# The eigen-solver beside an LSTM: rank-two vector formed in PSUM, shorter roots, counting by one instruction, selection by one-hot products

## The reference

```python
h = relu(layernorm(x)); x = x + L0(h, adj)   # A_hat h, W1, batch norm, relu, W2, batch norm
h = relu(layernorm(x)); x = x + L1(h, adj)   # two graph convolutions, then LSTMs over windows of 1 to 4 nodes
h = relu(layernorm(x)); x = x + L2(h, adj)   # U (relu((U^T h) W1 + b1) W2 + b2)
h = relu(layernorm(x)); x = x + L3(h, adj)   # three convolutions with adj * adj

# the part of L2 that the change is about
deg = sum(A, 0) + sum(A, 1) - diag(A)
d = where(deg > 0, rsqrt(deg), 0)
_, U = eigh(d[:, None] * (diag(deg) - A) * d[None, :])      # all eigenvectors of a 64x64 symmetric matrix
```

## Time and profile before

| | us |
|---|---|
| median of 3 runs | 989.73 (988.24 to 990.09) |
| the profiled execution | 988.91 |
| its span, first to last instruction | 987.1 |
| busy in the span: PE, DVE, ACT, POOL | 856.1, 571.1, 518.7, 348.2 |
| mean granted clock of TensorE | 0.962 of full |

### The profile page before, as it was taken

The page is one execution under the profiler, slowest core; times in us unless marked ns, Lnnn a source line. Parts: engine busy times, 40 slices in busy tenths (PEclk is TensorE's granted clock), DMA queues, the critical chain, the costliest instruction groups (busy, mean ns, idle before and its releaser), DMA issues.

```text
span 987.1 us, 12434 instructions
## 1 busy us (share of the span) xinstructions
PE 856.1 (87%) x3721; PEld 565.4 (57%) x3721; DVE 571.1 (58%) x3070; ACT 518.7 (53%) x958; POOL 348.2 (35%) x412
## 2 busy tenths in 40 slices
PE   2687768599899989998698879778999999999998
PEld 1344433364568536774367534566758848848846
DVE  5899867779778986779887987105104204304101
ACT  0466456466666736665466545474564454544531
POOL 1233210246555644565556556562202202202000
PEclk9999979799999999999899989898999999999999
DMA  8000000000000000000000000000000100100101
GB/s 336 0 1 1 1 0 1 1 1 1 0 1 1 1 1 1 2 0 1 0 1 1 1 1 0 1 1 1 1 0 2 43 0 1 43 0 1 43 1 43
DMA packets 2963, 13.27 MB, mean 13 GB/s; under 512 B 464, under 2 KB 464, under 8 KB 2640
## 3 DMA queue, kind: packets, MB, share of 16 engines
q1 hardware_dynamic: 2896, 12.48, 3.1%
HBM read 8.28 MB, written 4.19 MB: 13 GB/s over the span
## 4 chain that ended last, share of the span: by engine, by line
PE 61%; DVE 29%; ACT 4%; POOL 3%; issue 2%; DMA 0%; SPq 0%; DVEq 0%; ACTq 0%; POOLq 0%
PE PS L450 60%; POOL BIG L979 2%; DVE ST L1657 2%; DVE stats L1629 2%; DVE X L1833 2%; DVE Fq L1439 1%; DVE seg L1440 1%; ACT T L798 1%; DVE mv L1636 1%; DVE stats L1608 1%; ACT T L854 1%; POOL sc L948 1%; DVE sc L1173 1%; DVE vcol L1170 1%; DVE S L1190 1%
## 5 line engine op out<-in xcount | busy, mean ns | idle before, releaser
L450 PE MATMUL PS<-BIG,wts 128*128 128x512 f32 (+2 forms) x952 | 344.8, 498 | 14.2 <-POOL BIG L979 10.8
L979 POOL TENSOR_TENSOR BIG<-BIG 128x256 f32<-128x256 f32 (+2 forms) x252 | 239.2, 956 | 171.8 <-ACT BIG L888 88.0
L450 PEld LDWEIGHTS PS<-BIG,wts 128*128 128x128 f32 x952 | 179.0, 193 | 138.2 <-issue 96.8
L888 ACT ACTIVATE BIG<-PS,lbias 128x256 f32<-128x256 f32 (+2 forms) x312 | 165.5, 559 | 115.8 <-PE PS L450 113.5
L450 PE MATMUL PS<-H,wts 128*128 128x256 f32 (+2 forms) x312 | 123.0, 498 | 10.8 <-POOL H L979 7.0
L1833 DVE TENSOR_TENSOR X<-X,PS 128x512 f32<-128x512 f32 x64 | 43.3, 680 | 138.2 <-PE PS L450 87.1
L790 ACT ACTIVATE BIG<-PS 128x1024 f32<-128x1024 f32 x64 | 65.6, 1024 | 88.4 <-PE PS L450 88.4
L450 PE MATMUL PS<-T,wts 128*128 128x512 f32 x192 | 103.1, 659 | 2.2 <-ACT T L790 1.8
L790 ACT ACTIVATE T<-PS 128x512 f32<-128x512 f32 x96 | 55.8, 594 | 92.0 <-PE PS L450 91.7
L798 ACT ACTIVATE T<-X,shift,rstd 128x128 f32<-128x128 f32 x192 | 78.4, 482 | 34.6 <-DVE shift L1645 34.6
L1852 DVE TENSOR_TENSOR T<-PS,wts 128x512 f32<-128x512 f32 x16 | 11.1, 692 | 142.8 <-PE PS L450 142.8
(11 more groups left out here) (313 smaller groups left out, 1262.1 us busy)
## 6 DMA issues: line engine op xcount, KB each, us to landing
X<-x_in SPq DMA_DIRECT2D x1, 4096.0 KB, 12.7
out<-X SPq DMA_DIRECT2D x16, 256.0 KB, 2.0
wts<-w_in SPq DMA_DIRECT2D x1, 3542.0 KB, 21.4
cst<-cst_in SPq DMA_DIRECT2D x1, 419.0 KB, 3.4
AA<-adj_in SPq DMA_DIRECT2D x2, 16.0 KB, 2.0
```

The costliest lines, as they stand in the source:

```text
L450: return nc.tensor.matmul(o, l, r, start=start, stop=stop)
L888: nc.scalar.activation(LB[:, q, {"i": I_, "g": G_, "f": F_, "o": O_}[g], 0:n], PS[:, 3 * q + rank[q] % 3, 0:n], ACT.Tanh if g == "g" else ...
L979: nc.gpsimd.tensor_tensor(out, a, b, op).then_inc(pool_set[q], 1)
```

## The change

- `reflection`: before, DVE scaled the pieces of the rank-two vector into four scalars (`c2`, `vnn`, `wc`, `g0`) and used them apart. Now it adds `tn` times the row to A v in PSUM, in place (`av`), and both the next row and the update of S read that. `update` takes `pn` for `wc`.
- Inverse roots (`small_root`, and the same polynomial in `norm_roots`): the guess is one operation, followed by one Newton-like step and one step of higher order: 5 operations on single columns instead of 6 after the guess, and in the layer norm 7 instead of 9 after a guess of one instead of two.
- Grid: the tree of six additions over `Z` is one `tensor_reduce` that reads `Z` with the shift index outermost (a step of 32 elements) into `counts`. In round 0 the comparison of all counts with all lanes (2048 columns), its reduction and a copy are gone: DVE makes two 128-column tiles (`ends`, `inside`), and PE multiplies `inside` with the counts (33 columns) besides the product of before; three more single-column steps follow on DVE.
- Several operands lie in PSUM (`e_sum`, `t5`, `zb_sum`), and single-column `tensor_tensor` and `scalar_tensor_tensor` operations become `tensor_scalar` with a pointer.
- `PACE_AV` and its sisters are new, so the small products stand elsewhere between the LSTM's matmuls.

```diff
@@ -219,10 +219,10 @@
 
 
 PACE = 3.6
-PACE_AV = 7.45
-PACE_GRID = [52.0, 39.5]
-PACE_TWIST = 37.0
-PACE_SCAN = 16
+PACE_AV = 6.6
+PACE_GRID = [46.0, 38.0]
...
@@ -504,7 +505,8 @@
                     yield PACE_GRID[n]
                     pe.wait_ge(grid_cnt, n + 1)
                     if n == 0:
-                        mm(eb(2)[:, 0:1], tmp[:, :], ones[:, 0:1]).then_inc(grid_sum, 1)
+                        mm(eb(2)[:, 0:M + 1], tmp2[:, :], counts[:, :])
+                        mm(eb(2)[:, M + 1:M + 2], tmp[:, :], ones[:, 0:1]).then_inc(grid_sum, 1)
                     else:
                         mm(eb(2)[:, 0:1], C("fold"), sc[:, 3:4]).then_inc(grid_sum, 1)
...
@@ -1140,6 +1142,21 @@
                 do(v.tensor_scalar(y.bitcast(I32), y.bitcast(I32), -1.0, float(0x5F3759DF), ALU.mult, ALU.add))
                 wait()
                 return (3.0, 12.0, 768.0)
+
+            ROOT_MAGIC = float(0x5F3359DF)
+            ROOT_C, ROOT_MID = 2.89, 1.8895053
+            ROOT_A, ROOT_B = -10.0 / 3.0 * ROOT_MID ** 2, 5.0 * ROOT_MID ** 4
+            ROOT_SCALE = -3.0 / (8.0 * ROOT_MID ** 5)
+
+            def small_root(x, y, m):
+
+
+                yield v.tensor_scalar(y.bitcast(I32), x.bitcast(I32), -0.5, ROOT_MAGIC, ALU.mult, ALU.add)
+                yield v.tensor_scalar(m, y, x, y, ALU.mult, ALU.mult)
+                yield v.tensor_scalar(y, m, -ROOT_C, y, ALU.add, ALU.mult)
+                yield v.tensor_scalar(m, y, x, y, ALU.mult, ALU.mult)
+                yield v.tensor_scalar(m, m, ROOT_A, m, ALU.add, ALU.mult)
+                yield v.tensor_scalar(y, m, ROOT_B, y, ALU.add, ALU.mult)
 
...
@@ -1206,7 +1223,7 @@
                 first = op(v.scalar_tensor_tensor(trail, eb(2)[:, 0:NODES - 1 - k], vn, trail, ALU.mult, ALU.add))
                 yield first
                 dve.wait_ge(hh_ops, first)
-                yield op(v.scalar_tensor_tensor(trail, row_of(k, True), wc, trail, ALU.mult, ALU.add))
+                yield op(v.scalar_tensor_tensor(trail, row_of(k, True), pn, trail, ALU.mult, ALU.add))
 
             def reflection(k):
                 m = NODES - 1 - k
...
-                need(got)
-                for c in (3.0, 12.0, 768.0):
-                    got = op(v.tensor_scalar(m_, y_, n2, y_, ALU.mult, ALU.mult))
+                for ins in small_root(n2, y_, m_):
+                    got = op(ins)
                     next(off, None)
                     need(got)
-                    got = op(v.tensor_scalar(y_, m_, -c, y_, ALU.add, ALU.mult))
-                    next(off, None)
-                    need(got)
-                need(op(v.tensor_scalar(beta, y_, sn2, -1.0 / 8192, ALU.mult, ALU.mult)))
+                for _ in off:
+                    pass
+                need(op(v.tensor_scalar(beta, y_, sn2, ROOT_SCALE, ALU.mult, ALU.mult)))
                 v.tensor_scalar(vcol[:, :], C("next")[:, k:k + 1], beta, xc, ALU.mult, ALU.add).then_inc(hh_v, 1)
                 v.tensor_scalar(Av, trail[:, 0:1], beta, ax, ALU.mult, ALU.add).then_inc(hh_v, 1)
                 need(op(v.tensor_scalar(x0, x0, beta, None, ALU.add)))
                 need(op(v.tensor_scalar(hd, x0, beta, guard, ALU.mult, ALU.max)))
                 need(op(v.reciprocal(nc_, hd)))
                 dve.wait_ge(hh_v, k + 1 + k + 1 - REFLECTED)
-                first = op(v.tensor_scalar(a0, x0, nc_, -1.0, ALU.mult, ALU.mult))
-                second = op(v.tensor_scalar(vn, vcol[:, :], nc_, -1.0, ALU.mult, ALU.mult))
+                op(v.tensor_scalar(a0, x0, nc_, -1.0, ALU.mult, ALU.mult))
+                op(v.tensor_scalar(vn, vcol[:, :], nc_, -1.0, ALU.mult, ALU.mult))
                 op(v.tensor_scalar(pn, Av, nc_, -1.0, ALU.mult, ALU.mult))
-                need(first)
-                op(v.tensor_scalar(c2, a0, nc_, -1.0, ALU.mult, ALU.mult))
-                need(second)
-                op(v.tensor_scalar(vnn, vn, nc_, -1.0, ALU.mult, ALU.mult))
                 small_product()
                 dve.wait_ge(hh_av, k + 1)
-                t = eb(2)[:, m:m + 1]
-                if k + 1 < REFLECTIONS:
-                    got = op(v.tensor_scalar(w0, eb(2)[:, 0:1], nc_, -1.0, ALU.mult, ALU.mult))
-                    need(got - 1)
-                    op(v.tensor_scalar(wc, vnn, t, pn, ALU.mult, ALU.add))
-                    need(got)
-                    got = op(v.tensor_scalar(g0, c2, t, w0, ALU.mult, ALU.add))
-                    op(v.tensor_scalar(vr[:, 0:1], vr[:, 0:1], beta, None, ALU.add))
-                    need(got)
-                    need(op(v.scalar_tensor_tensor(urow[:, 0:m - 1], xr[:, 1:m], g0, eb(3)[:, 0:m - 1],
-                                                   ALU.mult, ALU.add)))
+                av, t = eb(2)[:, 0:m], eb(2)[:, m:m + 1]
+                last = k + 1 == REFLECTIONS
+                if not last:
+                    op(v.tensor_scalar(w0, av[:, 0:1], nc_, -1.0, ALU.mult, ALU.mult))
+                op(v.tensor_scalar(tn, t, nc_, -1.0, ALU.mult, ALU.mult))
+                got = op(v.tensor_scalar(vr[:, 0:1], vr[:, 0:1], beta, None, ALU.add))
+                if not last:
+                    need(got - 2)
+                    op(v.scalar_tensor_tensor(urow[:, 0:m - 1], xr[:, 1:m], w0, eb(3)[:, 0:m - 1], ALU.mult, ALU.add))
+                need(got - 1)
...
-                e, d, ne2, ne, t4, t5 = (Trow[:, n, :] for n in range(6))
+                e, d, ne2, ne, t4 = (Trow[:, n, :] for n in range(5))
+                e_sum, t5 = eb(0)[:, 0:NODES], eb(1)[:, 0:NODES]
                 step(v.tensor_copy(Trow[:, 0:2, :], eb(0)[:, 0:P].rearrange("p (a n) -> p a n", a=2)))
                 step(v.tensor_scalar(ne, e, -1.0, None, ALU.mult))
-                step(v.tensor_tensor(ne2, ne, e, ALU.mult))
+                step(v.tensor_tensor(ne2, ne, e_sum, ALU.mult))
                 step(v.tensor_scalar(ne2, ne2, -TINY, None, ALU.min))
 
...
-                        gsync()
-                        w //= 2
+                    gop(v.tensor_reduce(cn, Z[:, 0:NODES, :].rearrange("p i m -> p m i"), AX, ALU.add))
+                    gsync()
                     if r == 0:
 
-                        seen = Z[:, 0:NODES, :]
-                        gop(v.tensor_tensor(seen, cn.unsqueeze(1).broadcast_to([P, NODES, M]),
-                                            C("lanes").unsqueeze(2).broadcast_to([P, NODES, M]), ALU.is_le))
-                        gsync()
-                        gop(v.tensor_reduce(tmp[:, 0:NODES], seen, AX, ALU.add))
-                        gsync()
-                        busy(2 * PASS)
-                        v.tensor_copy(tmp[:, NODES:P], tmp[:, 0:NODES]).then_inc(grid_cnt, 1)
+                        lanes = C("lanes").unsqueeze(1).broadcast_to(pair)
+                        ends, inside = (t[:, :].rearrange("p (b n) -> p b n", b=2) for t in (tmp, tmp2))
+                        gop(v.tensor_scalar(ends, lanes, cn[:, M - 1:M], None, ALU.is_ge))
+                        gop(v.tensor_scalar(s1(6), s1(2), -float(M), s1(1), ALU.mult, ALU.add))
+                        gsync(1)
+                        v.scalar_tensor_tensor(inside, lanes, cn[:, 0:1], ends, ALU.is_ge, ALU.subtract)\
+                            .then_inc(grid_cnt, 1)
                     else:
                         v.tensor_scalar(xg[:, :], cn, C("lane"), None, ALU.is_le, ALU.add, accum_out=s1(3))\
                             .then_inc(grid_cnt, 1)
                     small_product()
                     dve.wait_ge(grid_sum, r + 1)
-                    gop(v.scalar_tensor_tensor(s1(1), eb(2)[:, 0:1], s1(2), s1(1), ALU.mult, ALU.add))
+                    if r == 0:
+                        gop(v.tensor_scalar(xg[:, :], eb(2)[:, 0:M], C("lane"), None, ALU.is_le, ALU.add,
+                                            accum_out=s1(3)))
+                        gsync()
+                        gop(v.tensor_scalar(s1(3), eb(2)[:, M:M + 1], float(M), s1(3), ALU.mult, ALU.add))
+                        gsync()
+                        gop(v.tensor_scalar(s1(3), eb(2)[:, M + 1:M + 2], float(M), s1(3), ALU.mult, ALU.add))
+                        gsync()
+                        gop(v.tensor_scalar(s1(1), s1(3), s1(2), s1(6), ALU.mult, ALU.add))
+                    else:
+                        gop(v.scalar_tensor_tensor(s1(1), eb(2)[:, 0:1], s1(2), s1(1), ALU.mult, ALU.add))
                     gsync()
...
                 step(v.tensor_tensor(zb, zb, zt, ALU.add))
-                step(v.tensor_tensor(zb, zb, hot, ALU.subtract))
-
-
-                step(v.tensor_tensor_reduce(junk[:, :], zb, zb, 1.0, 0.0, ALU.mult, ALU.add, s1(16)))
-                step(v.tensor_tensor_reduce(junk[:, 0:HALF], zb[:, 0:HALF], zb[:, 0:HALF], 1.0, 0.0, ALU.mult, ALU.add,
+                zb_sum = eb(1)[:, 0:NODES]
...
-                for c in inverse_root(s1(16), s1(29), step, lambda: None):
-                    step(v.scalar_tensor_tensor(s1(30), s1(29), s1(29), s1(16), ALU.mult, ALU.mult))
```

(18 more changed lines are left out.)

49 lines of the change are left out of this document (26 added, 23 removed).

## The result

The changed kernel takes 980.43 us (median; 977.20 to 981.85, 4 runs), the kernel before 989.91 us in the same measurement (988.24 to 990.92, 4 runs): ratio 0.9901, 95% interval 0.9873 to 0.993. That is faster by 9.5 us where 974 us, some 16 less, was forecast. The profiled execution took 981.11 us, its span is 979.2.

The account below looks back on a forecast made before the run. The LSTM stage was taken as a race of two fixed orders, PE's and DVE's: reflections 206 + solver 162 + rest 87 = 455 against 470.8 us, 16 less, so 974 us median; range 963 to 989.

Parts of the forecast that it names:

- Reflections, 206: Thirty-one reflections at the stage's start: 203.9 us at 6.6 each, plus 2 us of waits; DVE needs 5.9 each.
- rival A: Reflections: PE's new pace is too fast, PE waits at every product; 9 us net slower, 998 us; 10%.
- First grid product, 42: Solver piece up to the grid's first count: PE 42 us with the product, DVE 39, so no wait.
- The wait for ACT T: PE's 4.3 us wait near the fourth group's layer norm goes, because its root chain moves to the second round's recursion.
- Second grid product, 41 with a wait of 6: Solver's second grid round: PE 35 us of columns, DVE 40.6, so a new PE wait of about 6.
- The root chain, 2: Fourth group's layer-norm root within the second grid round: 2 us of DVE, standing behind steps of 0.16 us.
- Third, fourth, tail: 41, 15, 19: Solver's last pieces: both_ways 41 us, its 4.15 wait staying or growing; V 15; five-product tail 19, without L1 instructions.
- Rest, 87: LSTM work behind the solver: now 51 us for 23,840 columns, plus 36 for the 20,544 wide-round columns moved there.
- rival B: Behind the solver ACT and POOL bound the LSTM: 2.14 ns a column, rest 95 us, 14 of 16 lost, 988; 17%.
- Rival C: Grid's strided reduction costs more than 2.3 us: at twice the price 976 us, at four times 985; 11%.
- Rival D: Everything recovered: 17 us of PE waits and some 10 of half-clock stretches go, none comes: 962 us; 11%.
- The stretched steps: Two-operand DVE steps between both_ways and V become one-SUM-tensor steps: half the stretch credited, 1.7 us; the skill suggested all.

Follow-up runs that it names:

- e1: The kernel before with only the change's five new pace numbers, all old DVE instructions kept: 991.08 us, ratio 1.0018 to the kernel before.
- e2: The changed kernel with the five old pace numbers, so new work in the old order: 977.12 us, ratio 0.9867 to the kernel before.
- e5: The kernel before, old pace numbers, with only the grid's part of the change (one reduction, one-hot selection): 984.94 us, ratio 0.9949.
- e9: The kernel before, old pace numbers, with only the layer norm's root shortened, in all four groups: 987.37 us, ratio 0.9973.
- e7: The changed kernel with the fourth group's layer-norm root chain kept in PSUM, one instruction more: 978.08 us, ratio 0.9885 to the kernel before.
- e8: The changed kernel at the old pace numbers, with both_ways (42 for 37) and the last EV product (8.0 for 3.6) later: 966.05 us, ratio 0.9767.
- e4: The changed kernel with the old tree of six additions in place of the strided reduction, in both rounds: 979.98 us, ratio 0.9897.
- e11: The run at 966.05 us (new work, old pace, two products later) with the last group's norm chain also in PSUM: 967.59 us, ratio 0.9771.
- e12: The changed kernel, last group's norm chain in PSUM, third product's pace 41 for 36, last EV product's 8.0 for 3.6: 977.09 us, ratio 0.9857.

## Why the prediction was right, and where it was not

**The time.** Faster, as forecast, inside the range and inside the likeliest case's own; 6 us less than forecast. By its own steps:

- *Reflections, 206:* 209.2 (200.3 to 409.5). DVE had time left, as argued. DVE's line behind the reflections' products in the kernel after, answering to the earlier trace rows (its count, durations, first and last start; and its idle time and times):
```profile
L1282 DVE TENSOR_SCALAR sc<-PS,sc x30: 201/217/220, 201.2 to 400.5; 128x1 f32<-128x1 f32 x30
...
  PE PS L451: 34.5, 18
```
  29 periods in 199.3 us are 6.87 each, less 34.5/29 = 1.19 of waiting: DVE needs 5.7, forecast 5.9. PE's waits for S are 5.9 us in all, so rival A is out.
- *First grid product, 42:* 44.7 (409.5 to 454.2), without a wait of PE, as forecast.
- *The wait for ACT T:* gone as forecast (0.3), and the move that was given as the reason does remove it: it is gone in e1 too, where only the pace numbers are new. But it is not the only way. In e2 the chain stands where it stood and the wait is 0.9 us, in e5 1.8, in e9 2.0. "What moves is worth more than what goes" is the sentence that failed: the moves by themselves (e1) make the kernel slower, the shorter work by itself (e2) brings the gain.
- *Second grid product, 41 with a wait of 6:* 47.2 with a wait of 7.0. This is the mis-sized term. DVE needed 46.5 us for it (454.8 to 501.3), forecast 40.6. "The root chain, 2", and "inside 4 us" in the list of signs, rested on the claim that between steps of 0.16 us its steps would be short; six of them were stretched, by 5.5 us together (6.47 less six of 0.165). The reduction added 1.3. e7 takes the stretch away, and its piece is 41.4 (456.1 to 497.5) with a wait of 1.3. PE's own part was 40 instead of 35: 34.6 for the columns, 3.7 of two waits for POOL, and 1.7 for a stretch at half clock. The forecast had both only as a lump of 4 us for all pieces. So the 41 that e7 shows is PE's 40 and a short wait, not the forecast's 35 and 6.
- *Third, fourth, tail: 41, 15, 19:* 38.6, 14.1, 20.7. The wait at both_ways was to stay or grow and is 1.5; DVE catches up while PE stands at the second product, for in e7, where that wait is 1.3, the one at both_ways is 4.8. The tail still has its wait of 4.0, though no layer-norm instruction stands in it: the refinement's own chain is longer than its distance on PE. A pace of 8.0 removes it (e8).
- *Rest, 87:* 87.5 (574.8 to 662.3), or 1.97 ns a column, just under the 2 that was to be the sign of rival B; the 95 us that B wanted did not come.
- *Sum, 455:* 462.0. Of the 7 us, 6 are the second grid product; the rest spreads.

**Rival C,** the strided reduction: 3.69 us, 1.6 times the contiguous one of 2.29. Its price is real, and above the "near 2.3" of the list of signs. Against the tree it does no harm: the tree, 1 us dearer a round, gives the same time (e4).

**Rival D,** everything recovered (962 us), had 11%. It did not come, but e8 at 966 shows that nearly all of it was there to be had: with the new work at the old pace and two products later. The change gets 9.5 of e8's 24 us: the work is there, the distances are not.

**The stretched steps.** The prediction credited half, by rows that show the spread only for steps with two SBUF inputs. The rows above show it for steps with one as well: L1598 and L1614, SBUF to SBUF, 1.11 and 1.07 us. The trace of the kernel before had such a step too, beside a POOL product:
```profile
353.75 1.27 POOL L979 TENSOR_TENSOR BIG<-BIG 128x512 f32<-128x512 f32 x1
...
353.92 1.12 DVE L1138 TENSOR_SCALAR lnv<-lnv 128x16 int32<-128x16 int32 x1
```
Each such step ends with a product of POOL, and in e7, with an operand or the result in PSUM, a step inside such a product is as short as elsewhere. That the two engines share a way into SBUF is the reading of these rows, not something that they show by themselves.
On single columns, where the credit was given, half was too little: before, four steps between both_ways and V were stretched (4.2 us together), and in the kernel after no single-column step there takes over 0.28 us, so all of the stretch went, as the prediction had it by the Trainium skill.
The Trainium skill (SBUF — State Buffer, Who interferes with whom) says that VectorE's second pair of ports is GpSimd's; that two SBUF inputs need its read side; and that a `tensor_scalar` may use it too, in its two-port modes. The prediction had left out this last condition. The trace agrees on both kinds. It also says that `tensor_reduce` never contends on trn2, and the reduction is 3.69 and 3.61 us here, a spread of 2%.

## What to carry to other kernels

When one engine works a fixed list, add up its idle stretches and half of the time that it works at half clock, before and after: if they give the difference, a saving on another engine counts only where that engine was waited for. Before the parts of a change are added up, check that together they are the change. After work has been taken off, set the distances anew by looking at each product that still waits, and look at what takes the wait's place; room for one wait is a gain only if the instructions that move with it are not waited for themselves. Closing the distances because the work became shorter gave back part of the gain here (9.5 us between e11 and e12), while leaving them and widening two gave more than double the gain of the change.
